# Gating a layer's output by Silu: Silu through Tanh, with VectorE offsetting and gating at the end of each batch and GpSimd adding x

## The reference

```python
xn = _layernorm(x, axis=-1)
# attention branch, mlp(x) = gelu(x @ W1 + b1, exact) @ W2 + b2
q, k, v = mlp_q(xn), mlp_k(xn), mlp_v(xn)
scores = einsum('bid,bjd->bij', q, k) / sqrt(256 * 512) * tril(ones)
out = einsum('bij,bjd->bid', scores, v)
s = (out - mean(out)) * rsqrt(var(out) + 1e-5) * ln_w + ln_b
# feed-forward branch, weights quantised to -1, 0, 1
h = relu(xn @ Wq1.T + b1)            # 256 -> 1024
g = silu(h @ Wq2.T + b2)             # 1024 -> 256
x = x + s * g
```

## Time and profile before

| | us |
|---|---|
| median of 3 runs | 309.36 |
| lowest, highest | 308.67, 310.17 |
| the profiled execution: its time | 308.97 |
| its span, first to last instruction | 307.2 |
| busy: PE, PEld | 301.1, 270.5 |
| busy: DVE, ACT, POOL | 246.6, 221.2, 134.6 |

### The profile page before, as it was taken

How to read it: one execution, slowest core, us unless ns; L and a number is a source line. 1 busy time by engine, 2 the same in 40 slices (tenths; PEclk the granted TensorE clock), 3 DMA queues, 4 the chain that set the end, 5 groups by cost and what they waited for, 6 DMA issues and landing times.

```text
span 307.2 us, 5721 instructions
## 1 busy us (share of the span) xinstructions
PE 301.1 (98%) x1868; PEld 270.5 (88%) x1868; DVE 246.6 (80%) x540; ACT 221.2 (72%) x420; POOL 134.6 (44%) x104
## 2 busy tenths in 40 slices
PE   8999999999999999999999999999999999999994
PEld 8878899889988899888997889888998889988893
DVE  4889797967989588976989669895789858696686
ACT  3696948966786857949489576877579594795862
POOL 3945835168060942429151580608515292404100
PEclk9999999999999999999999999999999999999999
DMA  7960034420006000240005100060000500020001
GB/s 226 376 220 2 0 112 152 134 85 2 1 2 205 0 0 0 57 148 0 0 0 152 53 0 0 0 202 3 0 0 20 186 0 0 0 70 2 0 2 68
DMA packets 15228, 19.06 MB, mean 62 GB/s; under 512 B 1776, under 2 KB 12528, under 8 KB 15216
## 3 DMA queue, kind: packets, MB, share of 16 engines
q1 hardware_dynamic: 14656, 18.51, 18.9%
q10 hardware_dynamic: 560, 0.40, 0.4%
HBM read 14.69 MB, written 4.22 MB: 62 GB/s over the span
## 4 chain that ended last, share of the span: by engine, by line
PE 89%; DVE 4%; DMA 3%; SPq 1%; ACT 1%; issue 1%; POOL 0%; DVEq 0%
PE bank L830 89%; DMA x_all<-in_w1t 3%; DVE g_lo L642 1%; SPq L195 1%; DVE gw L748 1%; DVE gw L634 0%; DVE w1q L587 0%; DVE x_all L636 0%; ACT r_lo L398 0%; DVE gw L777 0%; PE bank L814 0%; SPq L206 0%; DVE s L585 0%; DVE y L754 0%; POOL o_rstd L357 0%
## 5 line engine op out<-in xcount | busy, mean ns | idle before, releaser
L724 DVE TENSOR_TENSOR r_lo<-bank,r_hi 128x512 fp32r<-128x512 f32 x64 | 44.0, 691 | 34.8 <-ACT bank L461 34.7
L460 ACT ACTIVATE r_hi<-bank,col 128x512 fp32r<-128x512 f32 x64 | 47.1, 735 | 24.0 <-PE bank L830 24.0
L357 POOL TENSOR_TENSOR o_rstd<-o_var,neg_half 128x2 f32<-128x2 f32 x16 | 11.2, 701 | 81.2 <-ACT o_var L484 81.2
L316 POOL TENSOR_TENSOR y<-y,xn 128x512 f32<-128x512 f32 x12 | 20.5, 1711 | 57.2 <-DMA y<-in_x_t 57.2
L461 ACT ACTIVATE bank<-bank,col 128x512 f32<-128x512 f32 x64 | 45.5, 711 | 0.0
L830 PE MATMUL bank<-xT_hi,w1q 128*128 128x512 f32 x128 | 39.7, 392 | 0.0
L830 PE MATMUL bank<-xT_lo,w1q 128*128 128x512 f32 x128 | 39.7, 392 | 0.0
L468 ACT CAST s_hi<-s 128x512 fp32r<-128x512 f32 (+3 forms) x32 | 14.7, 461 | 30.8 <-DVE s L712 28.0
L830 PE MATMUL bank<-w2q,r_lo 128*128 128x256 f32 x256 | 35.0, 279 | 0.0
L439 ACT ACTIVATE g_hi<-bank,col 128x512 fp32r<-128x512 f32 x48 | 34.0, 707 | 1.0 <-PE bank L830 0.9
L830 PE MATMUL bank<-w2q,r_hi 128*128 128x256 f32 x256 | 34.3, 276 | 0.0
(11 more groups left out here) (140 smaller groups left out, 700.7 us busy)
## 6 DMA issues: line engine op xcount, KB each, us to landing
out<-x_all SPq DMA_DIRECT2D x15, 256.0 KB, 3.1
x_all<-in_x SPq DMA_DIRECT2D x7, 512.0 KB, 3.6
xn<-x_norm_rows SPq DMA_DIRECT2D x6, 512.0 KB, 4.1
y<-in_x_t SPq DMA_DIRECT2D x6, 512.0 KB, 4.8
x_all<-in_w1t SPq DMA_DIRECT2D x2, 512.0 KB, 7.9
x_all<-in_w2t SPq DMA_DIRECT2D x1, 1024.0 KB, 10.4
row<-in_rows SPq DMA_DIRECT2D x1, 512.0 KB, 4.3
x_all<-in_x SPq DMA_DIRECT2D x1, 256.0 KB, 3.2
```

What stands on the lines that cost most here:

```text
L316: nc.gpsimd.tensor_tensor(half, half, x_mean_all, ALU.subtract).then_inc(xT_centred, 1)
L357: nc.gpsimd.tensor_tensor(o_rstd[:, half], o_var[:, half], neg_half[:, half], ALU.pow).then_inc(o_rstd_made, 1)
L460: nc.scalar.activation(r["hi"][:, f], pre[:], ACT.Relu, bias=b1)
L724: nc.vector.tensor_tensor(r["lo"][:, f], bank[(AT_F1 + f) % BANKS][:], r["hi"][:, f].bitcast(FP32), ALU.subtract).then_inc(r_split, 1)
```

## The change

1. ScalarE computes `th = tanh(y / 2)` into a tile of its own where it computed Silu in place. Since silu(y) = y/2 (1 + tanh(y/2)), VectorE makes `u = (th + 1) * y`, twice Silu(y) (`halve`), in one instruction, and the factor 1/2 goes into `ln_w` and `ln_b`, which ScalarE halves once, in batch 0.
2. The addition of `ln_b` (`offset`) moves from GpSimd to VectorE in every batch.
3. Both halves are gated (`gate`) at the end of their own batch; nothing of it is left in the next one.
4. GpSimd adds the gated halves to x (`add_x`) once both are gated, in all batches but the last, where VectorE still does it. The power for the next statistics (L267) stands before them.
5. The four bn_stats for the batch after next move from the batch's end into the `r_lo` stage, one behind each of the second to the fifth `r_lo`, in the loop's batches.

```diff
+        th = sb("th", [P, TT, C])
 ... (GpSimd, end of batch)
-                def offset(h):
-                    pool.wait_ge(o_read, 4 * i + 2 * h + 2)
-                    nc.gpsimd.tensor_tensor(gw[:, half], gw[:, half], row[:, ROW_LNB:ROW_LNB + 1].broadcast_to((P, 2, C)),
-                                            ALU.add).then_inc(s_made, 1)
+                def add_x(h):
+                    half = slice(2 * h, 2 * h + 2)
+                    nc.gpsimd.tensor_tensor(x_all[:, i, half], x_all[:, i, half], gw[:, half], ALU.add).then_inc(out_made, 1)
                 o_rstd_of(0)
                 o_rstd_of(1)
+                if not (second_last or last):
+                    x_rstd_of(i + 2)
                 if not last:
-                    offset(0)
-                    offset(1)
-                    if not second_last:
-                        x_rstd_of(i + 2)
+                    pool.wait_ge(s_gated, 2 * i + 2)
+                    add_x(0)
+                    add_x(1)
 ... (ScalarE)
                 if first:
+                    nc.scalar.mul(row[:, ROW_LNW:ROW_LNB + 1], row[:, ROW_LNW:ROW_LNB + 1], 0.5).then_inc(row_halved, 1)
-                def silu(t, tiles, ready):
+                def tanh(t, tiles, ready):
                     act.wait_ge(y_read, ready)
-                    nc.scalar.activation(y[:, t:t + tiles], y[:, t:t + tiles], ACT.Silu).then_inc(silu_made, 1)
+                    nc.scalar.activation(th[:, t:t + tiles], y[:, t:t + tiles], ACT.Tanh, scale=0.5).then_inc(tanh_made, 1)
 ... (VectorE: finish() goes, also from behind g_lo(1); r_lo stage)
                 for f in range(FT):
                     r_lo(f)
+                    if not (first or second_last or last) and 1 <= f <= TT:
+                        x_tile_stats(i + 2, f - 1)
+                def halve(t, tiles, n):
+                    dve.wait_ge(tanh_made, 2 * i + n)
+                    nc.vector.scalar_tensor_tensor(y[:, part], th[:, part], 1.0, y[:, part],
+                                                   ALU.add, ALU.mult).then_inc(u_made, 1)
+                def gate(t, tiles, n):
+                    dve.wait_ge(s_made, 2 * i + (1 if t == 0 else 2))
+                    dve.wait_ge(u_made, 2 * i + n)
+                    nc.vector.tensor_tensor(gw[:, part], gw[:, part], y[:, part], ALU.mult).then_inc(s_gated, 1)
 ... (VectorE, end of a loop batch)
                     y_bias(AT_Y0, 0, 2, 3 * i + 1)
                     y_bias(AT_Y1, 2, 1, 3 * i + 2)
-                        x_statistics(i + 2)
+                        x_statistics(i + 2, made=True)
+                    halve(0, 2, 1)
+                    dve.wait_ge(out_made, 2 * i)
                     o_scale(0)
+                    offset(0)
+                    gate(0, 2, 1)
                     y_bias(AT_Y2, 3, 1, 3 * i + 3)
                     o_scale(1)
-                    finish(i, 0, 2, 1)
+                    offset(1)
+                    halve(2, 2, 2)
+                    gate(2, 2, 2)
```

More of the change, by code:

```diff
@@ L547, in x_statistics @@
                 dve.wait_ge(x_norm_stored, 16 * b - 32)
-                for t in range(TT):
-                    nc.vector.bn_stats(x_stats[:, t], x_all[:, b, t]).then_inc(x_stats_made, 1)
+                if not made:
+                    for t in range(TT):
+                        x_tile_stats(b, t)
                 aggregate(x_stats, x_part, x_mean, x_var, x_stats_made, STEPS * (b - 2) + TT, x_var_made)
@@ L629, in batch @@
             def batch(i, first=False, second_last=False, last=False):
[L630 to L637, removed]
                 def g_lo(p):
@@ L757, in y_bias @@
                                             ALU.add).then_inc(y_read, 1)
[L759 to L762, removed]
+                def halve(t, tiles, n):
+                    part = slice(t, t + tiles)
+                    dve.wait_ge(tanh_made, 2 * i + n)
+                    nc.vector.scalar_tensor_tensor(y[:, part], th[:, part], 1.0, y[:, part],
+                                                   ALU.add, ALU.mult).then_inc(u_made, 1)
@@ new lines, in offset @@
+                def offset(h):
+                    half = slice(2 * h, 2 * h + 2)
+                    dve.wait_ge(o_read, 4 * i + 2 * h + 2)
+                    nc.vector.tensor_tensor(gw[:, half], gw[:, half],
+                                            row[:, ROW_LNB:ROW_LNB + 1].broadcast_to((P, 2, C)),
+                                            ALU.add).then_inc(s_made, 1)
+                def gate(t, tiles, n):
+                    part = slice(t, t + tiles)
+                    dve.wait_ge(s_made, 2 * i + (1 if t == 0 else 2))
+                    dve.wait_ge(u_made, 2 * i + n)
+                    nc.vector.tensor_tensor(gw[:, part], gw[:, part], y[:, part], ALU.mult).then_inc(s_gated, 1)
@@ new lines, in add_x @@
+                def add_x(t, tiles, n):
+                    part = slice(t, t + tiles)
+                    dve.wait_ge(s_gated, 2 * i + n)
+                    nc.vector.tensor_tensor(x_all[:, i, part], x_all[:, i, part], gw[:, part],
+                                            ALU.add).then_inc(out_made, 1)
+                if first:
+                    y_bias(AT_Y0, 0, 2, 3 * i + 1)
+                    y_bias(AT_Y1, 2, 1, 3 * i + 2)
+                    x_statistics(i + 2)
+                    dve.wait_ge(row_halved, 1)
+                    o_scale(0)
+                    xT_lo(1, [bank[(AT_X1 + k) % BANKS][:] for k in range(CK)])
+                    y_bias(AT_Y2, 3, 1, 3 * i + 3)
+                    o_scale(1)
+                    halve(0, 2, 1)
[4 more added lines that the diff above has]
+                    gate(2, 2, 2)
+                elif not last:
+                    xT_lo(i + 1, [xT32[:, k] for k in range(CK)])
+                    dve.wait_ge(xT_split, 2 * i + CK + 4)
@@ L765, in batch @@
                     if not second_last:
-                        x_statistics(i + 2)
+                        x_statistics(i + 2, made=True)
+                    halve(0, 2, 1)
+                    dve.wait_ge(out_made, 2 * i)
                     o_scale(0)
-                    if first:
-                        xT_lo(1, [bank[(AT_X1 + k) % BANKS][:] for k in range(CK)])
+                    offset(0)
+                    gate(0, 2, 1)
                     y_bias(AT_Y2, 3, 1, 3 * i + 3)
                     o_scale(1)
-                    finish(i, 0, 2, 1)
-                else:
[L774 to L779, removed]
+                    offset(1)
+                    halve(2, 2, 2)
+                    gate(2, 2, 2)
+                else:
                     y_bias(AT_Y0, 0, 2, 3 * i + 1)
+                    halve(0, 2, 1)
+                    dve.wait_ge(out_made, 2 * i)
                     o_scale(0)
                     offset(0)
-                    finish(i, 0, 2, 1)
+                    gate(0, 2, 1)
+                    add_x(0, 2, 1)
                     y_bias(AT_Y1, 2, 1, 3 * i + 2)
```

29 lines of the change are left out of this document (19 added, 10 removed).

## The result

The changed kernel takes 309.96 us (median of 20 runs, 309.53 to 310.79), the kernel before 308.90 in the same comparison (20 runs). The ratio is 1.0032, 95% interval 1.0024 to 1.0040: 1.0 us slower, 0.7 to 1.2. The forecast was +1.15 and 310.5. Executions more than 1.5% above the fastest of their kernel (three of the kernel before, two of e5) are left out of every ratio here. The profiled execution took 309.76, its span 307.9 us.

A forecast was written before the change was run, and what follows sets the result against it. TensorE was taken to bound the kernel, with VectorE's chain bounding the program's end. Terms -0.5 + 1.65 = +1.15 us gave 310.1 from the profiled 308.97, or 310.5 for the median; range 309.2 to 312.3.

The forecast's parts named there:

- TensorE's waits: At `g_lo` and the second batch's start: removing the table loads saves what TensorE waited, -0.5 us.
- The table of Tanh: On ScalarE: one load left in the program's list, fifteen of 1.28 us gone, although the skill's page suggested loads would stay.
- third rival: Table loads stay: last batch's Tanh ends 1.3 us later, TensorE gains nothing, 312.3 us; chance 3%.
- VectorE at the end of a loop batch: Added `halve` and `offset` work there doesn't delay K; cost 0, upper bound +0.6 us.
- fourth rival: Batch ends, batch 0's or others', run later than counted; K or banks wait, +0.5 to +2 us; chance 9%.
- GpSimd's additions: Behind `gate`, two of about 1.3 us delay the store and next x^T load; nothing on TensorE's path waits.
- bn_stats between the `r_lo`: In the `r_lo` stage, each bn_stats fits VectorE's 0.47 us idle gap; cost 0.
- second rival: In the `r_lo` stage GpSimd holds up the bn_stats, +10 us, 320 us in all; chance 6%.
- The last batch: Three terms on VectorE's chain at the program's end, +1.65 us together, bounds +1.4 to +2.0.
- `halve` ahead of `o_scale`: Last batch: `halve` of tiles 0 and 1 stands before `o_scale` and delays its start, +0.52 us.
- from there to the end: Last batch, from the start of tile 3's bias to the end: 2.30 us instead of 2.00, +0.30 us.
- second term: Last batch, between tiles 2 and 3's offset and tile 3's bias: an added `halve` and gate, +0.83 us.

The follow-up runs named there:

- e5: e1 with the last batch's table load issued early and GpSimd adding x for tiles 0 and 1 there; ratio 0.9988 to the kernel before.
- e9: e1 with tile 3's bias again ahead of tile 2's gating in the last batch; ratio 0.9983 to the kernel before.
- e2: Kernel before with Tanh in place of Silu, so only the table loads go (computes another function); ratio 0.9998 to the kernel before.
- e8: Changed kernel with Silu where it has Tanh, so the table loads return (computes another function); ratio 1.0300 to the kernel before.
- e4: Changed kernel with the four bn_stats back at the batch's end; ratio 1.0034 to the kernel before.
- e6: Changed kernel with eight extra bn_stats, 2.7 us of VectorE work, at the end of batches 1 to 6; ratio 1.0181 to the kernel before.
- e7: Changed kernel with GpSimd adding tiles 0 and 1 as soon as they are gated; ratio 1.0068 to the kernel before.
- e3: Kernel before with only the changed kernel's new end in the last batch; ratio 1.0053 to the kernel before.
- e1: Changed kernel with Silu in place and no `halve` in the last batch; ratio 1.0000 to the kernel before.
- e10: e5 with tile 3's bias again ahead of tile 2's gating in the last batch; ratio 0.9984 to the kernel before.

## Why the prediction was right

- *TensorE's waits, -0.5 us.* Right in kind. V's start lost 0.10 and doesn't any more, and the second batch's first two matmuls no longer lose theirs. The size is less sure: e9 measured -0.5 (0.2 to 0.9), e2 at most -0.3, the profiles -0.35 to -0.55, of which 0.2 is a difference that isn't the waits (last section). I had named the loads and the gating as joint causes; taking the loads away is enough (e2), and the gating's part was not tested.
- *The table of Tanh.* One load in the whole trace. Tanh and Gelu run from the same table here, and a load took 1.28 us with no further pause. The Trainium skill, page "ScalarE: Activation LUTs", section "Table sets: the hidden batching unit", lists Gelu in a set without naming tanh; the trace doesn't agree, as its one load shows. What loads would cost with the new order (third rival, +1.3 and no gain) I put far too low: e8 measured +9.3. The step that failed there is the wait: in the new order VectorE's head instruction waits for the first function in each batch, and I had that in the last batch alone.
- *VectorE at the end of a loop batch, 0.* Right. `gate` ended at 89.17, on the old clock 89.5, where I had said 89.8, and the room before K was 2.0 us (1.6 said). e4 and e6 bound it: 1.4 us more is free, 2.7 is not. After batch 0 the room was 0.55 us (0.4 said), so the fourth rival, a late end of batch 0, falls too; e7 shows how little was left.
- *GpSimd's additions, 0.* Right, because they wait for both pairs. e7 shows what that wait is for.
- *bn_stats between the `r_lo`, 0.* Right; the second rival falls with the row at 105.64, without an experiment of its own.
- *The last batch.* +1.65 forecast, +1.49 in the profile, +1.6 in e3. By terms, each counted as in the forecast: `halve` ahead of `o_scale` +0.31 (0.52 said), up to the bias of tile 3 +0.86 (0.83), from there to the end +0.32 (0.30). The first was mis-sized since `halve` took 0.69, not 0.742: with both operands in SBUF it ran like a two-operand instruction, and 0.61 from start to start. And Tanh followed the small activation at once, 0.14 us sooner than the load had, counted from the batch's first matmul. In the third two errors cancelled, which is luck: `halve` took 0.43 where I had 0.47, and the pause between it and its gate was 0.10 where I had 0.03 to 0.04.
- *The median.* 310.5 was forecast and 309.96 measured. Nearly all of the 0.5 us is the base: 309.36 was the median of 3 runs, and 20 runs of the same kernel have 308.90.

Not seen beforehand: a quarter to a third of the last batch's growth (0.3 to 0.5 us, e1 against e9) comes from the order of gating and bias, not from the work added. The forecast had it inside its second term without telling the two apart.

## What to carry to other kernels

Removing 19 us of loads from an engine that held TensorE up by a few tenths gave about 0.5 us, and three short instructions and one changed order on the chain behind the last matmul took it back three times over. Look at the program's end by itself: there, the form that is cheapest in the loop can be the wrong one, and it is cheap to keep another (e9). When an engine's work is rearranged, measure its room as the distance to the next reader, batch by batch, the first one included.

## What the runs showed of the hardware

- VectorE and GpSimd held each other up in both directions, and only where VectorE had two operands in SBUF: `halve` 1.79 and the offset 1.53 instead of 0.69 behind an addition on GpSimd (e7), and GpSimd's power over two values per partition 1.22 instead of 0.70 us behind a gating (e5). The changed kernel has it too, where nobody waits for it: the same power took 1.04 us at the end of its second batch, behind an offset. bn_stats and `r_lo`, with one operand in SBUF, kept their times beside `v_lo`. This agrees with the Trainium skill, page "SBUF — State Buffer", section "Who interferes with whom".
- TensorE's matmul rate differs a little between stretches with no wait: batch 1 took 36.22 us in six profiles with nothing to wait for, the changed kernel's among them, and 36.01 in e1 and e10, at the same granted clock of 1.00. All of the 0.21 us arises before V (V starts 11.20 us into the batch instead of 10.99), where the matmuls of the first products start 0.233 us apart instead of 0.229. I don't know the cause. It is as large as half of what the loop gained.
